# Two scores per step drained by ScalarE, and more columns raised by GpSimd, in a fourth-power attention on one core

## What is computed

```python
s = jnp.einsum('bhtd,bhsd->bhts', q, k)
s = s - s.mean(axis=-1, keepdims=True)
mad = jnp.abs(s).mean(axis=-1, keepdims=True) + 1e-06
s = s / mad * score_gain
s = jnp.where(causal[None, None], s, jnp.asarray(-1000.0, s.dtype))
r = jnp.maximum(s, 0.0) ** POWER          # POWER = 4
att = r / (r.sum(axis=-1, keepdims=True) + 1e-06)
y = jnp.einsum('bhts,bhsd->bhtd', att, v)
```

## Time and profile before

| | us |
|---|---|
| median of 3 runs | 1008.33 (1005.89 to 1010.31) |
| the profiled execution | 1009.18 |
| its span | 1007.4 |
| PE busy over the span | 875.2 (87%) |
| DVE busy | 706.8 (70%) |
| ACT busy | 566.1 (56%) |
| POOL busy | 446.6 (44%) |

### The profile page before, as it was taken

One profiled execution on the slowest core, in us unless ns is written; L12 is line 12 of the kernel. 1 busy time (PEld: TensorE's weight loads), 2 busy tenths in 40 slices (PEclk: granted clock), 3 DMA queues, 4 the chain that ended last, 5 costly groups with the idle time before them and its releaser, 6 DMA issues.

```text
span 1007.4 us, 18333 instructions
## 1 busy us (share of the span) xinstructions
PE 875.2 (87%) x6003; PEld 443.6 (44%) x6010; DVE 706.8 (70%) x1486; ACT 566.1 (56%) x655; POOL 446.6 (44%) x884
## 2 busy tenths in 40 slices
PE   6699999999999977679993898899999998988890
PEld 4222232232232344449992454343433334367790
DVE  6778988988988678734543579677888786545346
ACT  4488898898898732122221530365665665846571
POOL 3145554554553560047884330134333343625773
PEclk8599999999999999979997657599999999989896
DMA  5401011011030041216765333741331114221433
GB/s 181 137 1 48 1 48 47 0 47 47 0 88 1 3 147 31 58 32 165 200 137 104 110 110 96 180 96 52 98 94 52 48 49 149 64 77 42 123 96 104
DMA packets 74064, 79.74 MB, mean 79 GB/s; under 512 B 14904, under 2 KB 60824, under 8 KB 70520
## 3 DMA queue, kind: packets, MB, share of 16 engines
q1 hardware_dynamic: 65008, 67.51, 22.3%
q0 software_dynamic: 8128, 9.84, 4.7%
q10 hardware_dynamic: 864, 1.57, 0.4%
HBM read 57.23 MB, written 21.68 MB: 78 GB/s over the span
## 4 chain that ended last, share of the span: by engine, by line
PE 60%; DVE 22%; issue 7%; ACT 4%; POOL 4%; DMA 2%; DVEq 0%; SPq 0%; ACTq 0%; POOLq 0%
PE acc_ps L842 12%; PE acc_ps L1206 7%; DVE mx L571 7%; PE tail_ps L1143 5%; PE causal_ps L1186 5%; PE causal_ps L1372 4%; PE causal_ps L804 4%; DVE R L1756 3%; POOL moe_rows L2515 2%; PE causal_ps L815 2%; PE causal_ps L1383 2%; DVE tails L1762 2%; PE causal_ps L1040 2%; PE tail_ps L1040 2%; PE tail_ps L804 1%
## 5 line engine op out<-in xcount | busy, mean ns | idle before, releaser
L1610 ACT ACTIVATE EX<-causal_ps 128x1024 f32<-128x1024 f32 (+1 forms) x154 | 140.4, 938 | 137.9 <-PE causal_ps L1186 137.7
L571 DVE TENSOR_REDUCE mx<-tail_ps 128x1 f32<-128x512 f32 x266 | 158.1, 632 | 46.0 <-PE tail_ps L1146 33.2
L1468 ACT ACTIVATE R<-R 128x2048 f32<-128x2048 f32 (+1 forms) x80 | 134.9, 1740 | 0.5 <-DVE R L1756 0.5
L1143 PE MATMUL tail_ps<-KM,QM 72*128 72x512 bf16 (+1 forms) x320 | 106.8, 355 | 6.5 <-DVE mx L571 2.3
L2557 POOL TENSOR_TENSOR pacer<-eps_ln 128x1 f32<-128x1 f32 x140 | 27.1, 193 | 187.4 <-ACT EX L1610 187.0
L1756 DVE TENSOR_SCALAR R<-causal_ps 128x1024 f32<-128x1024 f32 (+1 forms) x88 | 93.8, 1074 | 20.1 <-PE causal_ps L804 18.6
L1762 DVE TENSOR_REDUCE tails<-causal_ps 128x1 f32<-128x768 f32 (+4 forms) x96 | 93.4, 973 | 14.6 <-PE causal_ps L815 12.9
L1475 ACT ACTIVATE R<-R 128x1792 f32<-128x1792 f32 (+4 forms) x80 | 100.7, 1271 | 0.0
L1186 PE MATMUL causal_ps<-QE,KE 75*128 75x512 bf16 (+3 forms) x369 | 98.7, 339 | 0.8 <-ACT EX L1610 0.4
L2365 POOL TENSOR_TENSOR R<-R 128x512 f32<-128x512 f32 (+2 forms) x64 | 86.0, 1359 | 1.3
L1206 PE MATMUL acc_ps<-EX,VS 128*32 128x512 f32 (+3 forms) x768 | 82.9, 507 | 0.9 <-DVE EX L2274 0.6
(11 more groups left out here) (411 smaller groups left out, 1676.9 us busy)
## 6 DMA issues: line engine op xcount, KB each, us to landing
QS<-q_parts SPq DMA_DIRECT2D x8, 576.0 KB
KS<-k_parts SPq DMA_DIRECT2D x24, 192.0 KB
QM<-q_parts SPq DMA_DIRECT2D x8, 576.0 KB
KM<-k_parts SPq DMA_DIRECT2D x24, 192.0 KB
QE<-q_parts SPq DMA_DIRECT2D x8, 576.0 KB
KE<-k_parts SPq DMA_DIRECT2D x24, 192.0 KB
wg<-in_wg_t SPq DMA_DIRECT2D x16, 256.0 KB, 2.9
wu<-in_wu_t SPq DMA_DIRECT2D x16, 256.0 KB, 3.3
```

The source lines that it names most:

```text
L571: return reduce(mx[:, par, hh, o0:o0 + step * (cnt - 1) + 1:step], scores[:, 0:cnt * w].rearrange("p (c w) -> p c w", w=w), AX.X, op, **how)
L1143: mm = pe.matmul(slot[:, at:at + w], QM[0:ROWS, par, hh, i * P:(i + 1) * P], KM[0:ROWS, par, hh, k0:k0 + w], start=True, stop=not diag, sk ...
L1468: act.activation(R4[:, rp, h0:h0 + 2, 0:width], R1[:, rp, h0:h0 + 2, 0:width], ACT.Square).then_inc(squared, 1)
L1610: act.activation(EX[:, rp, hh, 0:width], slot[:, 0:width], ACT.Exp, scale=float(D) ** -0.5).then_inc(exp_done, 1)
```

## The change

It adds a table of the score jobs that ACT drains, c1 and c2 in steps 0 to 2, and c2 alone in steps 3 and 4, and a table of the columns of the first piece that POOL raises: 384, 384, 256, 128 and 384 in place of 128 in each. ACT raises the rest. Nothing else moves: PE fills the same jobs in the same order.

```diff
-BY_ACT = [kind == "c" and n == ACT_HEAD for _, kind, n in JOBS]
+ACT_HEADS = [(1, 2), (1, 2), (1, 2)] + [(2,)] * (NS - 3)
+BY_ACT = [kind == "c" and n in ACT_HEADS[s] for s, kind, n in JOBS]
+POOL_FIRST = [3 * P, 3 * P, 2 * P, P, 3 * P]
...
-                act.wait_ge(filled, NJ * g + RELU_AT[s, ACT_HEAD] + 1)
-                act.activation(R1[:, rp, ACT_HEAD, 0:width], slots[SLOT[RELU_AT[s, ACT_HEAD]]][:, 0:width],
-                               ACT.Relu).then_inc(drained_act, 1)
+                for hh in ACT_HEADS[s]:
+                    act.wait_ge(filled, NJ * g + RELU_AT[s, hh] + 1)
+                    act.activation(R1[:, rp, hh, 0:width], slots[SLOT[RELU_AT[s, hh]]][:, 0:width],
+                                   ACT.Relu).then_inc(drained_act, 1)
...
-                act.activation(R4[:, rp, h0:h0 + 2, P:n], R4[:, rp, h0:h0 + 2, P:n], ACT.Square
+                lo = POOL_FIRST[s]
+                act.activation(R4[:, rp, h0:h0 + 2, lo:n], R4[:, rp, h0:h0 + 2, lo:n], ACT.Square
...
-                        cols = slice(at, at + (width if n else P))
+                        cols = slice(at, at + (width if n else POOL_FIRST[s]))
```

## The result

Five runs of the changed kernel gave a median of 1023.35 us (1017.65 to 1024.78), five of the kernel before 1009.19 (1005.89 to 1010.31). The ratio on record (it isn't that of the two medians) is 1.0133, with a 95% interval of 1.0108 to 1.0159. So the kernel is slower, by 14 us where 5.65 were forecast, and its time lies outside the range given, 1004 to 1018.

A forecast was written before the change was run, and what follows sets the result against it. It took PE, waiting on ACT's queue at step 2's u7, to set the time, not DVE's load: 7 x 0.80 + 0.25 - 0.2 = +5.65 us, giving 1014.0 us against the 1008.33 median; own range 1011.5 to 1016.5, wider range 1004 to 1018.

The forecast's parts named there:

- ACT's sum from c2 to c1: ACT's queue from step 1's c2 to step 2's c1, without idle time: 8.26 us, so that drain starts at 210.44.
- PE's wait: Step 2, before u7: PE idle about 1.4 us in seven quads until ACT has drained c1.
- ended by line 1458: Sign in step 2: PE's idle before the fill at line 817 is ended by ACT's keep at line 1458.
- the gain of step 1: Step 1: with c1 off DVE, PE's fill of c3 starts at about 202.45 instead of 203.09, 0.64 us earlier.
- Step 0's c1: Step 0: moving this drain off DVE gains nothing, since DVE then waits longer for the fill of u2.
- exclusion of the two: POOL and DVE sharing an SBUF port: full exclusion would add up to 2.6 us a quad, some 20; forecast took zero.
- u7 starts at 211.52 instead of 210.72, 0.80 us later: Step 2: u7 waits for ACT's drain of c1; nothing takes the delay back, so each quad is 0.80 us longer.
- The end: Last quad: POOL's last columns ready at 346.1, end at 347.1, +0.25 us beyond the counted 0.80 (up to +0.8).
- POOL's step 2: POOL's step 2 multiplication ends at 222.5; PE needs it at 222.40 plus 0.80, so hidden by 0.7.
- Rival A: Not slower: DVE bounds, step 2's c1 doesn't hold u7, 0.64 us gained in every quad: 1003.8 us; chance 0.15.
- the first half clock: First quad: the clock is half up to about 56 us, so PE is slower and doesn't wait at u7.
- first quad: First quad, without a wait at u7: -0.2 us, bounds -0.6 and +0.8.

The follow-up runs named there:

- step1_early: Changed kernel with only step 1's c1 moved to ACT, drained between step 0's squares, POOL columns 384, 128, 128, 128, 128: 1004.38 us, ratio 0.9949 to before.
- heads01_p0: Changed kernel with step 2's c1 back on DVE and POOL columns 384, 128, 128, 128, 128: 1007.88 us, ratio 0.9975 to before.
- pool_not1: Changed kernel with ACT draining c2 alone in every step and POOL columns 384, 128, 256, 128, 384: 1012.23 us, ratio 1.0016 to before.
- refill: Changed kernel with step 2's c2 filled three more times by PE right ahead of the waiting u7: 1017.31 us, ratio 1.0081 to before.
- pool_only: Changed kernel with ACT draining c2 alone in every step, POOL's wide columns kept: 1014.67 us, ratio 1.0043 to before.
- heads01: Changed kernel with step 2's c1 back on DVE, steps 0 and 1 and POOL's wide columns kept: 1014.15 us, ratio 1.0042 to before.
- head_step2: Changed kernel with only step 2's c1 moved to ACT, POOL's wide columns kept: 1020.19 us, ratio 1.0078 to before.
- early_c1: Changed kernel with step 2's c1 drained on ACT between step 1's squares, POOL columns 384, 128, 128, 128, 128: 1009.47 us, ratio 0.9979 to before.
- refill1: Changed kernel with step 2's c2 filled one more time by PE ahead of u7: 1016.78 us, ratio 1.0061 to before.

## Why the prediction failed

**What held.** The chain and ACT's order of time put the cost at the right place and in the right size. ACT's sum from c2 to c1 was 8.26 us, as predicted; PE's wait 1.43 for 1.4; the quad 38.55 for 38.5; ended by line 1458. step1_early and heads01_p0 showed the gain of step 1 to be real, up to 0.80 a quad for 0.64, and lost in the changed kernel as described. Step 0's c1 was worth nothing, and DVE and POOL were busy as summed. No exclusion of the two was seen: in pool_not1, with 4.3 us more of POOL's work, DVE is busy 33.45 us a quad for 33.51.

**The step that failed** is "u7 starts at 211.52 instead of 210.72, 0.80 us later ... each quad is 0.80 longer". The wait of 1.4 us was priced at its length alone, 0.80 a quad net of step 1's gain. No sentence of the prediction says what an idle time of 1.4 us does to the granted clock of the matmuls behind it: it was neither bounded nor made a rival, though the profile lists that clock in every window. refill, which changes only whether PE is idle in the wait, gave 38.55 us in all quads and 1017.31; with the idle time it was 1023.35 and 1022.32. A low stretch of 3.4 us costs 1.5, one of 10.2 us 4.7; in the two profiles they sum to 4.5 and about 9.3. Of the 9.3 us by which the median lies above the forecast this is some 6, 1023.35 less refill's 1017.31. The other 3.3 are the 0.6 of the end (below), the kernel before itself (its three runs of the forecast had a median of 1008.33, the 22 runs beside refill one of 1009.89), and time behind the attention (663.0 us in refill's profile, 661.3 before); how they share it is only roughly known.

**Two smaller ones.** The end was forecast at 0.25 beyond the wait, and in refill it was 0.87: I left POOL's last multiplication on the time scale of before (346.1) while shifting PE by 0.80. Before, POOL went from step 3 to step 4 without a pause. In refill it is free earlier, as assumed, but stands idle 0.87 us for ACT's squares, which follow a fill of PE's. And POOL's step 2, "hidden, by 0.7", was hidden only behind the loss: the forecast was right for this kernel, but pool_only shows that this part of the change costs 0.28 a quad when nothing else does. Rival A's 1003.8 rested on all of the gain showing once u7 is free; heads01 had u7 free and a quad of 38.03, so its condition was incomplete. One reading was off without effect: the first half clock ended at 53.9 us, not at about 56.

With these terms the sum nearly closes: 5.6 (seven waits) + 0.9 (end) - 0.3 (first quad) = 6.2, where refill's 352.39 less 346.09 is 6.3; in the changed kernel come low stretches of 4.5 and 9.3, less a first quad that was some 1.5 shorter than refill's (refill fills over again there too).

**What stays open.** Behind the attention the span has between 660 and 667 us in kernels that are the same there (661.3 before, 665.0 in pool_only, 666.0 in head_step2 and heads01, 666.7 in early_c1). Stretches of the low clock lie in it at changing places and lengths. In the profiles of head_step2 and heads01 it is 4.7 us longer than before, a large part of what their medians are above the time expected. What decides it wasn't tried. Nor is it known why one idle time of 1.43 us is followed by a low stretch and the next, just as long, isn't.

## To carry to other kernels

Before a drain is moved to another engine, sum that engine's queue from its last real wait to the new instruction, and compare with when the buffer is next filled; here the place in the queue (0.8 us a quad) counted for more than the work (early_c1 has more of it and is faster). A new idle time of TensorE isn't priced by its length alone: look at what the granted clock does behind it, and if the wait must be, filling it with harmless matmuls can be cheaper than standing still. A gain ahead of such a wait only makes the wait longer. And where one part of a change delays everything, its other parts are hidden; each must be costed again without that cover.

## What was not expected of the hardware

Seven times in each of the two profiles of the changed kernel PE stood idle for 1.43 us, with work before and after. Behind seven of these fourteen the granted clock fell to 0.50, from 0.6 to 1.8 us after the wait had ended, and stayed there for 3.4 us or, once, 10.2. Which of them it follows differs from run to run. Behind the idle times of 0.63 us (head_step2) and 1.00 us (refill1) at the same place it fell in no quad of their profiles.
